# A fused attention and slot-router kernel: two thirds of the encoder's values multiplied behind the first tile, and the row sum moved to GpSimd

## The chip, the cores and the metric

One core of a Trainium2 chip runs the whole program. The metric is the device time of one execution in microseconds. Three executions of the kernel before were timed, and one execution was taken by the hardware profiler. TensorE (PE in the profile) multiplies matrices, VectorE (DVE), ScalarE (ACT) and GpSimd (POOL) work on tiles, SyncE (SP) issues most of the transfers. Each engine works through its own program in the written order and waits for the others only through semaphores.

## The reference

The inputs are 8 batches of 512 rows of 512 numbers (`x`), encoder rows of the same shape (`ctx`), a position `p` and a length for each batch. Everything is float32. Two residual blocks follow one another:

```python
# block 1: attention on a window of the encoder
h = (x - mean(x)) / sqrt(var(x) + 1e-5)
score = einsum('nqh,hk,nlk->nql', h, W_a, enc)
score = where(idx < max(p-16, 0) or idx > min(p+16, len), -1e9, score)
align = softmax(score) * exp(-(idx - p)**2 / 128)
context = einsum('nql,nlh->nqh', align, enc)
x = x + tanh(concat([context, h]) @ W_c.T)
# block 2: a router to 64 slots, on h2 = layernorm(x)
logits = (gelu(concat([h2, slot_mean]) @ w1 + b1) @ w2 + b2) / (abs(tau) + 0.1)
alpha  = softmax over the 8 largest logits, scattered into 64 slots
si     = einsum('bts,btd->bsd', alpha, h2) / (alpha.sum(1) + 1e-8)
S_new  = GRU(si, slots); attention among the slots; layernorm; @ wvp
x = x + einsum('bts,bsd->btd', alpha, slot_values) @ wo + bo
```

Only 36 encoder rows of a batch can count (34 of the window and two more columns for the case that nothing is masked in), so the kernel gathers these. In block 1 it multiplies the weights into the encoder once: `G` = window rows times `W_a`, so that a score is a product of `h` and `G`; and `EW` = window rows times the left half of `W_c`, times the Gauss weight, so that the context's part of the tanh is the product of softmax weights and `EW`. These are the encoder values of the title. The right half of `W_c` (`Wc2_raw`, which the profile calls Wc_raw) is multiplied with `h` directly, and since `h` has its mean taken off, the mean over the rows of this half is taken off the weights instead: `wcs` is the sum of its four pieces of 128 rows, and one product with a constant matrix `cmean` (-1/512 everywhere) gives minus the row mean for all partitions.

## The kernel before

The program is written by hand for each engine; no scheduler moves anything. Float32 products are made as three products of rounded parts: `mm3` multiplies high by high, low by high and high by low (the lines 456 to 458 of the profile). A high part is a rounding copy, usually on ScalarE; a low part is a subtraction of the high part from the full one, usually on VectorE (`..._lo`). The low parts that matter here are `WaT_lo` (weights of G, one operation for each of the four pieces of 128 rows), `Wc1T_lo` (weights of `EW`), `G_lo`, `GW_lo` (the second weights that a tile is multiplied with) and `EW_lo`.

Ahead of the tiles TensorE makes, in this order: the G products (48, piece k = 0 to 3 outermost, each k waits for `encWT` to say that `WaT_lo` of that piece is there), the product of the mean, and 36 products for `EW` in three groups `g` of 12. Group g holds the windows of batches 3g to 3g+2. VectorE meanwhile makes the `WaT_lo`, the three sums of `wcs`, the four `Wc1T_lo`, the four `G_lo`, adds the mean's product to the four pieces of `Wc2_raw`, splits the first tile (`low_x(0)`, the tile called hT_lo), and makes the four `GW_lo`.

Then come 32 tiles of 128 rows, in steps s = 0 to 31 on every engine. In step s TensorE makes the scores and the left half of the direct part (`score(s)`, 12 products with 292 columns), turns the softmax weights of tile s-1 (`turn_weights`, L1795), makes the right half (`right_half(s)`, 12 products with 256 columns), adds the context of tile s-1, does what `extras(s)` holds (in steps 1 to 6 the slots' own products) and turns the normalised rows of tile s-2 (`turn_rows`, L1770, which waits for `xh` of ScalarE). VectorE in step s takes the largest score, makes the statistics of tile s+3 (`stats1`), the softmax weights (`stack`), and the statistics of the new rows of tile s-1 (`stats2`). GpSimd adds the tanh to the row tile (`residual`), splits tile s+2 (`low_x`), makes the inverse deviations (`scales1`, `scales2`), and copies the four pieces of G of a batch beside the weights (`keys`). `w1` is the router's first weight matrix, which VectorE splits in step 1.

The semaphore `pre` counts what TensorE has finished ahead of the tiles. In the kernel before it stands at 1 after the hidden bias, at 2 to 5 after the four columns of G, at 6 after the mean and at 7 to 9 after the groups of `EW`. `EW` goes to its place for the context product by transfers: the first batch's three by ScalarE, after group 0, and the others by SyncE, which waits for `ew` to be 3, ahead of the loads of tiles 6 and later.

## Time and profile before

| | us |
|---|---|
| median of three executions | 347.88 |
| lowest and highest of them | 347.34, 349.73 |
| span of the profiled execution | 345.3 |
| TensorE busy (share of the span) | 328.8 (95%) |
| VectorE busy | 249.3 (72%) |
| ScalarE busy | 200.6 (58%) |
| GpSimd busy | 209.5 (61%) |
| mean granted TensorE clock | 0.992 of full |

The span runs from the first to the last instruction of the profiled execution. Its own device time is not listed apart from the three; by their median it would be the span and some 2.6 us around it. The start on the profile's clock is 0. In the rows below, a start and a duration are microseconds, `x4` says that four instructions stand in one row, and brackets at the end hold the idle time ahead of the row and what ended it.

### The profile page before, as it was taken

Reading aid. Unit: us, or ns where it says so; the run is one execution under the profiler, and the core shown is the slowest. Engines: PE = TensorE matmul, PEld = TensorE weight load, DVE = VectorE, ACT = ScalarE, POOL = GpSimd, SP = SyncE. Lnnn points to the kernel's source line nnn. Section 1 sums busy time; section 2 is a strip of 40 time slices with the busy share of each in tenths; the row PEclk is TensorE's granted clock in tenths of the full one; section 3 lists DMA queues with packets and bytes.
Section 4 is the critical chain, followed back from the end, with each engine's and each line's share of the span. In section 5 each row is a group of like instructions: output and inputs, shape, how many; then the busy total and the mean of one; then the engine's idle time right before and its main releaser. Section 6 shows DMA issues by size and latency. Waiting matters only on the chain.

```text
span 345.3 us, 7118 instructions
## 1 busy us (share of the span) xinstructions
PE 328.8 (95%) x2320; PEld 284.0 (82%) x2320; DVE 249.3 (72%) x749; ACT 200.6 (58%) x406; POOL 209.5 (61%) x353
## 2 busy tenths in 40 slices
PE   8999998999999999999999999989999999999980
PEld 6697856999898989989989989977889886777750
DVE  5589897666787777878877877766944765578872
ACT  3567226477759679578587777676853345323420
POOL 5600247879687876875885785737674336136772
PEclk9999999999999999999999999999999999999996
DMA  7999866242424242232232300009700000000898
GB/s 274 277 348 388 296 194 208 68 122 63 121 64 122 62 125 64 72 113 61 84 101 63 91 5 2 0 0 338 251 2 1 0 2 0 0 2 1 323 345 307
DMA packets 40934, 42.79 MB, mean 124 GB/s; under 512 B 3245, under 2 KB 32045, under 8 KB 40898
## 3 DMA queue, kind: packets, MB, share of 16 engines
q1 hardware_dynamic: 38944, 40.19, 35.2%
q10 hardware_dynamic: 1666, 1.49, 1.3%
q0 software_dynamic: 288, 0.66, 0.6%
q8 instruction: 19, 0.31, 0.4%
q14 instruction: 17, 0.14, 0.1%
HBM read 32.18 MB, written 8.39 MB: 117 GB/s over the span
## 4 chain that ended last, share of the span: by engine, by line
PE 57%; POOL 11%; DVE 9%; issue 8%; ACT 6%; DMA 6%; SPq 1%; POOLq 0%; ACTq 0%; DVEq 0%
PE psum L456 13%; PE psum L457 13%; PE psum L458 13%; PE psum L1741 4%; PE psum L2003 3%; POOL hT_lo L599 3%; DMA xT<-in_xT 3%; PE psum L1770 3%; DMA encw<-in_enc,rowi 2%; PE psum L1721 2%; POOL X L604 2%; ACT th L1320 2%; POOL r2all L610 1%; PE psum L1805 1%; PE psum L1952 1%
## 5 line engine op out<-in xcount | busy, mean ns | idle before, releaser
L456 PE MATMUL psum<-GW_hi,hT_hi 128*128 128x292 f32 (+1 forms) x256 | 78.5, 307 | 0.0
L458 PE MATMUL psum<-GW_lo,hT_hi 128*128 128x292 f32 (+1 forms) x256 | 73.9, 289 | 0.0
L457 PE MATMUL psum<-GW_hi,hT_lo 128*128 128x292 f32 (+1 forms) x256 | 73.9, 289 | 0.0
L604 POOL TENSOR_TENSOR X<-X,th 128x512 f32<-128x512 f32 x32 | 38.2, 1193 | 28.4 <-ACT th L1320 28.4
L456 PEld LDWEIGHTS psum<-GW_hi,hT_hi 128*128 128x128 f32 x256 | 48.4, 189 | 1.4 <-issue 1.2
L457 PEld LDWEIGHTS psum<-GW_hi,hT_lo 128*128 128x128 f32 x256 | 48.3, 189 | 0.0
L458 PEld LDWEIGHTS psum<-GW_lo,hT_hi 128*128 128x128 f32 x256 | 48.1, 188 | 0.0
L971 DVE BATCH_NORM_STATS2 st<-X 128x6 f32<-128x512 f32 x32 | 22.2, 693 | 26.7 <-POOL X L604 26.6
L599 POOL TENSOR_TENSOR hT_lo<-xT,hT_hi 128x512 fp32r<-128x512 f32 x30 | 39.1, 1304 | 2.0 <-DVE stack L982 2.0
L456 PE MATMUL psum<-xhT_hi,w_hi 128*128 128x256 f32 x128 | 37.9, 296 | 0.8 <-issue 0.5
L457 PE MATMUL psum<-xhT_hi,w_lo 128*128 128x256 f32 x128 | 36.1, 282 | 0.0
L458 PE MATMUL psum<-xhT_lo,w_hi 128*128 128x256 f32 x128 | 36.0, 281 | 0.0
L1307 ACT CAST aTs<-psum 108x128 fp32r<-108x128 f32 x32 | 8.6, 268 | 32.9 <-PE psum L1795 32.9
L1315 ACT ACTIVATE xh<-X,nm,r2all 128x512 f32<-128x512 f32 x31 | 25.1, 809 | 3.9 <-POOL nm L613 3.4
L456 PEld LDWEIGHTS psum<-xhT_hi,w_hi 128*128 128x128 f32 x128 | 24.2, 189 | 3.6 <-issue 3.4
L1301 ACT ACTIVATE e<-scm,nmr,rr 128x36 f32<-128x36 f32 x32 | 13.3, 417 | 20.0 <-DVE nmr L967 19.0
L457 PEld LDWEIGHTS psum<-xhT_hi,w_lo 128*128 128x128 f32 x128 | 24.3, 190 | 0.0
L458 PEld LDWEIGHTS psum<-xhT_lo,w_hi 128*128 128x128 f32 x128 | 24.3, 190 | 0.0
L456 PE MATMUL psum<-siT_hi,W_hi 128*128 128x256 f32 (+1 forms) x72 | 23.4, 325 | 0.0
L457 PE MATMUL psum<-siT_hi,W_lo 128*128 128x256 f32 (+1 forms) x72 | 23.1, 320 | 0.0
L458 PE MATMUL psum<-siT_lo,W_hi 128*128 128x256 f32 (+1 forms) x72 | 22.9, 318 | 0.0
L958 DVE TENSOR_TENSOR xhT_lo<-psum,xhT_hi 128x512 fp32r<-128x512 f32 x32 | 21.4, 667 | 2.0 <-ACT xhT_hi L1296 2.0
(316 smaller groups left out, 909.6 us busy)
## 6 DMA issues: line engine op xcount, KB each, us to landing
xT<-in_xT SPq DMA_DIRECT2D x32, 256.0 KB, 2.9
X<-in_x SPq DMA_DIRECT2D x32, 256.0 KB, 3.5
out<-ost SPq DMA_DIRECT2D x32, 256.0 KB, 3.0
WhhT<-in_WhhT SPq DMA_DIRECT2D x1, 3072.0 KB, 12.7
WihT<-in_WihT SPq DMA_DIRECT2D x4, 768.0 KB, 8.6
Wo<-in_wo ACTq DMA_DIRECT2D x4, 256.0 KB, 3.0
WvpT<-in_WvpT SPq DMA_DIRECT2D x4, 256.0 KB, 3.7
WaT<-in_WaT SPq DMA_DIRECT2D x1, 1024.0 KB, 11.1
```

Source lines behind the costliest of these rows:

```text
L456: pe.matmul(out, w_hi, m_hi, start=start, stop=False)
L457: pe.matmul(out, w_lo, m_hi, start=False, stop=False)
L458: return pe.matmul(out, w_hi, m_lo, start=False, stop=stop)
L599: pool.tensor_tensor(hT_lo[:, t % 2, :, :], xT[:, t % 4, :, :], hT_hi[:, t % 2, :, :].bitcast(F32), ALU.subtract).then_inc(S("hl"), 1)
L604: pool.tensor_tensor(tile_x(r), tile_x(r), halves(th[:, :]), ALU.add).then_inc(S("x2"), 1)
L958: v.tensor_tensor(xhT_lo[:, :, dst], bank.rearrange("p (c n) -> p c n", c=KC), xhT_hi[:, :, dst].bitcast(F32), ALU.subtract).then_inc(S("x ...
L971: link(v.bn_stats(st2[:, :], tile_x(r)), "stat")
L1301: act.activation(e[:, :], scm[:, :], ACT.Exp, bias=nmr[:, :], scale=rr1[:, s % 4:s % 4 + 1], accum_out=esum[:, :]).then_inc(S("ex"), 1)
L1315: act.activation(halves((th if r == NT - 1 else xh)[:, :]), tile_x(r), ACT.Identity, bias=nm2[:, :], scale=r2all[:, r:r + 1]).then_inc(S(" ...
L1741: last = pe.matmul(SI[h * NS:(h + 1) * NS, 0:XW], al, X[:, TPB * b + q, h, :], start=q == 0, stop=q == TPB - 1)
L1770: last = pe.transpose(bank[:, c * P:(c + 1) * P], rows_of[:, c * P:(c + 1) * P], ident[:, :])
L2003: last = pe.matmul(out_banks(m)[par], w[at_b, :], mv[g][at_b, :], start=n == 0, stop=n == 2)
```

## The change

Seven edits belong together.

1. TensorE makes the mean's product ahead of the last quarter of G. `pre` is therefore 2 after the mean and 3 to 6 after G's columns.
2. The three sums of `wcs` are made by GpSimd, which counts them in `row_sum`, followed by `low_x(0)`, which VectorE made.
3. VectorE adds the mean's product to `Wc2_raw` ahead of `G_lo`.
4. TensorE makes only group 0 of `EW` ahead of the tiles. Groups 1 and 2 (batches 3 to 7) are made in `extras(0)`, behind the right half of tile 0.
5. ScalarE and VectorE make `EW_hi` and `EW_lo` of these groups within step 0.
6. The wait for all of `GW_lo` ahead of step 0 is replaced by one for each piece within the first score.
7. ScalarE makes `w1_hi` at the end of its step 1, VectorE `w1_lo` in its step 2 (both were VectorE's in step 1).

```diff
-HB_DONE, G_DONE, WM_DONE, EW_DONE = 1, 1, KC + 2, KC + 2
+HB_DONE, WM_DONE, G_DONE, EW_DONE = 1, 2, 2, KC + 2
@@ gpsimd, behind the copy of bvz
+        pool.wait_ge(S("in_wc2"), 16)
+        pool.tensor_tensor(wcs[:, :], Wc2_raw[:, 0, :], Wc2_raw[:, 1, :], ALU.add).then_inc(S("row_sum"), 1)
+        for k in range(2, KC):
+            pool.wait_ge(S("row_sum"), k - 1)
+            pool.tensor_tensor(wcs[:, :], wcs[:, :], Wc2_raw[:, k, :], ALU.add).then_inc(S("row_sum"), 1)
+        low_x(0)
         pool.wait_ge(S("g_lo"), KC)
         keys(0)
@@ vector
-        v.wait_ge(S("in_wc2"), 16)
-        link(v.tensor_tensor(wcs[:, :], Wc2_raw[:, 0, :], Wc2_raw[:, 1, :], ALU.add), "rt")
-        link(v.tensor_tensor(wcs[:, :], wcs[:, :], Wc2_raw[:, 2, :], ALU.add), "rt")
-        v.tensor_tensor(wcs[:, :], wcs[:, :], Wc2_raw[:, 3, :], ALU.add).then_inc(S("v_prep"), 1)
@@
-        low_x(0)
@@ vector, extras
-            if s == 1:
-                v.wait_ge(S("in_w1"), 16)
-                link(v.tensor_copy(w1_hi[:, :, :], w1_raw[:, :, :]), "w1s")
-                link(v.tensor_tensor(w1_lo[:, :, :], w1_raw[:, :, :], w1_hi[:, :, :].bitcast(F32), ALU.subtract), "w1s")
+            if s == 2:
+                v.wait_ge(S("w1s"), 1)
+                v.tensor_tensor(w1_lo[:, :, :], w1_raw[:, :, :], w1_hi[:, :, :].bitcast(F32), ALU.subtract).then_inc(S("w1s"), 1)
@@ scalar, step
+            if s == 0:
+                high_values(1)
+                high_values(2)
+            if s == 1:
+                act.wait_ge(S("in_w1"), 16)
+                act.wait_ge(S("pre"), EW_DONE + NG)
+                act.copy(w1_hi[:, :, :], w1_raw[:, :, :]).then_inc(S("w1s"), 1)
@@ tensor
         for k in range(KC):
+            if k == KC - 1:
+                pe.wait_ge(S("row_sum"), ROW_SUM)
+                pe.wait_ge(S("wp"), KC)
+                pe.matmul(banks[7], cmean[:, :], wcs[:, :], start=True, stop=True).then_inc(S("pre"), 1)
@@
-        for g in range(NG):
+        def encoder_values(g):
@@
+        encoder_values(0)
+
         def extras(s):
 
+            if s == 0:
+                for g in range(1, NG):
+                    encoder_values(g)
@@ tensor, extras(2): the H1 bank; turn_rows(0): the trX bank
+                pe.wait_ge(S("ew"), 2)
+            if r == 0:
+                pe.wait_ge(S("ew"), NG)
@@ tensor, score
             for c in range(KC):
+                if s == 0:
+                    pe.wait_ge(S("split"), KC + c + 1)
@@
-        pe.wait_ge(S("split"), 2 * KC)
```

How the order changes on VectorE between `WaT_lo` and the first statistics: the tile names are the ones used above, and line numbers are those of each kernel. Before:

```order
L836 TENSOR_TENSOR wcs<-Wc_raw 128x512
L837 TENSOR_TENSOR wcs<-wcs,Wc_raw 128x512
L838 TENSOR_TENSOR wcs<-wcs,Wc_raw 128x512
L841 TENSOR_TENSOR Wc1T_lo<-Wc1T,Wc1T_hi 128x512 x4
L851 TENSOR_TENSOR G_lo<-psum,G_hi 128x288 x4
L856 TENSOR_TENSOR Wc_raw<-Wc_raw,psum 128x512 x4
L845 TENSOR_TENSOR hT_lo<-xT,hT_hi 128x512
L860 TENSOR_TENSOR GW_lo<-Wc_raw,GW_hi 128x512 x4
L864 SCALAR_TENSOR_TENSOR EW_lo<-psum,gw,EW_hi 108x512
L845 TENSOR_TENSOR hT_lo<-xT,hT_hi 128x512
```

The same place on VectorE in the changed kernel:

```order
L845 TENSOR_TENSOR Wc1T_lo<-Wc1T,Wc1T_hi 128x512 x4
L854 TENSOR_TENSOR Wc_raw<-Wc_raw,psum 128x512 x4
L859 TENSOR_TENSOR G_lo<-psum,G_hi 128x288 x4
L864 TENSOR_TENSOR GW_lo<-Wc_raw,GW_hi 128x512 x4
L868 SCALAR_TENSOR_TENSOR EW_lo<-psum,gw,EW_hi 108x512
L850 TENSOR_TENSOR hT_lo<-xT,hT_hi 128x512
```

The three sums and one `hT_lo` are gone, and the subtraction of the mean stands ahead of `G_lo`.

GpSimd behind its share of the weights of `Wp`. Before:

```order
L641 COPY bvz<-vecs 128x4
L585 COPY GW_hi<-G_hi 128x4x36
L586 COPY GW_lo<-G_lo 128x4x36
L593 TENSOR_SCALAR ve_168<-mr_167 128x2
L594 TENSOR_TENSOR rr_169<-ve_168,neghalf 128x2
```

GpSimd at the same place in the changed kernel:

```order
L643 COPY bvz<-vecs 128x4
L645 TENSOR_TENSOR wcs<-Wc_raw 128x512
L648 TENSOR_TENSOR wcs<-wcs,Wc_raw 128x512 x2
L601 TENSOR_TENSOR hT_lo<-xT,hT_hi 128x512
L587 COPY GW_hi<-G_hi 128x4x36
L588 COPY GW_lo<-G_lo 128x4x36
```

Four operations of 128x512 with two operands have come in ahead of the copies of `keys(0)`.

TensorE at the end of the encoder's products. Before, the last `G` product is followed by the mean, and the value products begin:

```order
L457 MATMUL psum<-encWT_hi,WaT_lo 128x288
L458 MATMUL psum<-encWT_lo,WaT_hi 128x288
L1624 MATMUL psum<-wcs,cmean 128x512
L456 MATMUL psum<-Wc1T_hi,encWT_hi 108x512
L457 MATMUL psum<-Wc1T_hi,encWT_lo 108x512
L458 MATMUL psum<-Wc1T_lo,encWT_hi 108x512
```

TensorE in the changed kernel, where group 0 of the values ends and the first tile's score begins:

```order
L458 MATMUL psum<-Wc1T_hi,encWT_hi 108x512
L459 MATMUL psum<-Wc1T_hi,encWT_lo 108x512
L460 MATMUL psum<-Wc1T_lo,encWT_hi 108x512
L458 MATMUL psum<-GW_hi,hT_hi 128x292
L459 MATMUL psum<-GW_hi,hT_lo 128x292
```

The score now follows after 12 value products, where it followed after 36, and the mean's product is no longer between G and the values.

## Rows read from the trace of the kernel before

**Rows 1.** The page, part 1: busy time, share and instructions of each engine.

```profile
PE 328.8 (95%) x2320; PEld 284.0 (82%) x2320; DVE 249.3 (72%) x749; ACT 200.6 (58%) x406; POOL 209.5 (61%) x353
```

**Rows 2.** Waits of TensorE from 20 to 64 us: total, times, longest.

```profile
PE psum L1770 <- ACT xh L1315: 1.2, 2, 1.0
PE psum L1795 <- DVE stack L982: 0.5, 1, 0.5
```

**Rows 3.** TensorE in order of time: start, duration, line, operation, out<-in.

```profile
20.91 0.38 PE L456 MATMUL psum<-encWT_hi,WaT_hi 128*128 128x288 f32 x1
...
27.36 1.02 PE L1624 MATMUL psum<-wcs,cmean 128*128 128x512 f32 x2
...
28.45 0.39 PE L457 MATMUL psum<-Wc1T_hi,encWT_lo 128*108 128x512 f32 x1
...
36.57 0.30 PE L456 MATMUL psum<-GW_hi,hT_hi 128*128 128x292 f32 x1
...
39.59 0.30 PE L456 MATMUL psum<-GW_hi,hT_hi 128*128 128x292 f32 x1
```

**Rows 4.** VectorE in order of time, 20 to 36 us, same columns.

```profile
21.23 0.74 DVE L810 SCALAR_TENSOR_TENSOR WaT_lo<-WaT,wneg,WaT_hi 128x512 fp32r<-128x512 f32 x1
...
24.73 0.69 DVE L838 TENSOR_TENSOR wcs<-wcs,Wc_raw 128x512 f32<-128x512 f32 x1
...
25.34 2.49 DVE L841 TENSOR_TENSOR Wc1T_lo<-Wc1T,Wc1T_hi 128x512 fp32r<-128x512 f32 x4
...
28.45 1.55 DVE L851 TENSOR_TENSOR G_lo<-psum,G_hi 128x288 fp32r<-128x288 f32 x4 [0.62 <-PE psum L1624]
...
29.92 2.47 DVE L856 TENSOR_TENSOR Wc_raw<-Wc_raw,psum 128x512 f32<-128x512 f32 x4
...
32.91 2.49 DVE L860 TENSOR_TENSOR GW_lo<-Wc_raw,GW_hi 128x512 fp32r<-128x512 f32 x4
```

**Rows 5.** ScalarE in order of time, 23 to 28 us.

```profile
23.95 2.19 ACT L1271 CAST Wc1T_hi<-Wc1T 128x512 fp32r<-128x512 f32 x4 [2.73 <-DMA Wc1T<-in_WcT]
...
26.08 0.62 ACT L1276 CAST hT_hi<-xT 128x512 fp32r<-128x512 f32 x1
```

**Rows 6.** The load of Wc_raw: its issue, and its row in the DMA issues.

```profile
15.17 0.37 SPq L494 DMA_DIRECT2D Wc_raw<-in_WcT  x1
...
Wc_raw<-in_WcT SPq DMA_DIRECT2D x1, 1024.0 KB, 5.5
```

**Rows 7.** VectorE beside GpSimd (POOL), at three later places.

```profile
242.65 0.43 DVE L1003 SCALAR_TENSOR_TENSOR kept<-kept,lsub 128x256 f32<-128x256 f32 x1
...
155.64 1.49 DVE L1003 SCALAR_TENSOR_TENSOR kept<-kept,lsub 128x256 f32<-128x256 f32 x1
...
155.56 1.29 POOL L599 TENSOR_TENSOR hT_lo<-xT,hT_hi 128x512 fp32r<-128x512 f32 x1
...
244.99 1.50 DVE L911 CAST W_hi<-WihT 128x512 fp32r<-128x512 f32 x1
...
246.16 1.46 POOL L660 TENSOR_TENSOR W_lo<-WihT,W_hi 128x512 fp32r<-128x512 f32 x1
```

**Rows 8.** VectorE from 41 to 51 us, and ScalarE's exponential of tile 3.

```profile
41.57 0.26 DVE L982 SCALAR_TENSOR_TENSOR stack<-e,ev,stack 128x36 f32<-128x36 f32 x1
...
48.00 1.81 DVE L929 CAST w_hi<-w_raw 128x1024 fp32r<-128x1024 f32 x1
...
49.84 1.23 DVE L930 TENSOR_TENSOR w_lo<-w_raw,w_hi 128x1024 fp32r<-128x1024 f32 x1
...
57.96 0.42 ACT L1301 ACTIVATE e<-scm,nmr,rr 128x36 f32<-128x36 f32 x1 [0.78 <-DVE nmr L967]
```

**Rows 9.** Busy time by stretch at the end; PEclk is 1.00 at 2.4 GHz.

```profile
core 0: us, PE busy (x) PEld busy (x) DVE busy (x) ACT busy (x) POOL busy (x), PEclk, DMA share, GB/s
337.00:339.00 2.00, 0.00 (x0) 0.00 (x0) 1.96 (x3) 0.69 (x1) 1.61 (x2) 1.00 1.04 392
340.00:345.00 5.00, 0.00 (x0) 0.00 (x0) 0.00 (x0) 0.00 (x0) 0.00 (x0) 0.50 0.68 263
```

More of the change, by code:

```diff
@@ L33 @@
 HT = T // 2
-HB_DONE, G_DONE, WM_DONE, EW_DONE = 1, 1, KC + 2, KC + 2
+HB_DONE, WM_DONE, G_DONE, EW_DONE = 1, 2, 2, KC + 2
 HI_WA, HI_ENC, HI_WC1, HI_G, HI_GW, HI_EW = 4, 4 + KC, 6 + KC, 6 + 2 * KC, 6 + 3 * KC, 6 + 4 * KC
 BVZ_DONE, LOW_WP = 5, 5
-SUMS_DONE, MEAN_DONE, CHUNKS_DONE, LOW_WC1 = 2, 3, 4, 4
+SUMS_DONE, MEAN_DONE, LOW_WC1 = 2, 3, 3
+ROW_SUM = 3
 SPLIT_WP = (2, 3)
@@ L844, in low_x @@
             v.wait_ge(S("hh"), t + 1)
+            v.wait_ge(S("hl"), t)
             v.tensor_tensor(hT_lo[:, t, :, :], xT[:, t, :, :], hT_hi[:, t, :, :].bitcast(F32), ALU.subtract).then_inc(S("hl"), 1)
+        v.wait_ge(S("pre"), WM_DONE)
+        for k in range(KC):
+            v.tensor_tensor(Wc2_raw[:, k, :], Wc2_raw[:, k, :], banks[7], ALU.add).then_inc(S("split"), 1)
         for c in range(KC):
@@ L851, in _ @@
             v.tensor_tensor(G_lo[:, c, :], src, G_hi[:, c, :].bitcast(F32), ALU.subtract).then_inc(S("g_lo"), 1)
-        v.wait_ge(S("pre"), WM_DONE)
-        for k in range(KC):
-            v.tensor_tensor(Wc2_raw[:, k, :], Wc2_raw[:, k, :], banks[7], ALU.add).then_inc(S("split"), 1)
-        low_x(0)
         for k in range(KC):
@@ L870, in _ @@
         stats1(1)
-        low_values(1)
         g3 = lambda a: a.rearrange("p (j s) -> p j s", s=NS)
@@ L1032, in step @@
                 scores_max(s)
-                if s == 0:
-                    low_values(2)
                 if live(s + 3) and s:
@@ L1039, in step @@
                     stats1(2)
+                    low_values(1)
             for b in range(NB):
@@ L1044, in step @@
                 stats1(3)
+                low_values(2)
             if s in TOPK_STEP:
@@ L1387, in _, with high_values @@
         act.wait_ge(S("first_row"), 1)
-        for g in range(NG):
-            if g == 2:
-                act.wait_ge(S("ew"), 1)
-                for k, part in enumerate((EW_hi, EW_hi, EW_lo)):
-                    act.dma_start(EW3[k * WS:(k + 1) * WS, 0, :].bitcast(F32),
-                                  part[0:WS, 0, :].bitcast(F32)).then_inc(S("ew3_first"), 16)
+        def high_values(g):
             act.wait_ge(S("pre"), EW_DONE + g + 1)
             act.activation(EW_hi[:, g, :], banks[4 + g][0:WP, :], ACT.Identity, scale=gw[0:WP, g:g + 1]).then_inc(S("wa"), 1)
+        high_values(0)
+        act.wait_ge(S("ew"), 1)
+        for k, part in enumerate((EW_hi, EW_hi, EW_lo)):
+            act.dma_start(EW3[k * WS:(k + 1) * WS, 0, :].bitcast(F32), part[0:WS, 0, :].bitcast(F32)).then_inc(S("ew3_first"), 16)
         for s in range(NT):
@@ L1620, in _ @@
                     last.then_inc(S("pre"), 1)
-        pe.wait_ge(S("v_prep"), CHUNKS_DONE)
-        pe.wait_ge(S("wp"), KC)
-        pe.matmul(banks[7], cmean[:, :], wcs[:, :], start=True, stop=True).then_inc(S("pre"), 1)
-        for g in range(NG):
+        def encoder_values(g):
             at_g = slice(g * WP, (g + 1) * WP)
```

## The prediction

> **What bounds the kernel now.** Read the shares of busy time first: TensorE is busy for 328.8 us of a span of 345.3 [rows 1]. Such a share says only that TensorE's work is nearly the whole time; what an edit is worth is decided by TensorE's idle time in the stretch that the edit touches. So I listed its waits from 20 to 64 us [rows 2]: three, 1.7 us in all. They are 0.5 us for the first tile's softmax weights and 1.2 us in two waits for the normalised rows `xh`, the longer one 1.0. Before 20.9 us the change moves nothing on TensorE, and it removes no product. The most that it can give back is therefore 1.7 us, 0.5%. What it can lose is open, because a step that had cover may lose it.
>
> Next, the order of time on TensorE [rows 3]. The products for G start at 20.91, one every (27.36 - 20.91) / 48 = 0.134 us. The mean's product starts at 27.36 and the 36 encoder value products follow, one every (36.57 - 28.45) / 35 = 0.232 us, which puts the mean's product at 28.45 - 0.23 - 27.36 = 0.86. The first score starts at 36.57 and step 0's 24 products end at 39.59, so they take 3.02 (score 1.61, right half 1.41). There is no idle time in all of this.
>
> Then VectorE over the same stretch [rows 4], where the columns to read are start and duration. It goes from one operation to the next, and its last `GW_lo` is done at 35.4, 1.2 us before TensorE comes to the score. The 8.4 us of encoder value products are the cover of this chain. That is the point on which the case turns.
>
> **The change part by part.**
>
> *24 of 36 value products behind the first tile.* The same work on TensorE, 24 x 0.232 = 5.57 us, comes later. TensorE now stands before the score at 36.57 - 5.57 = 31.0 and needs the four pieces of `GW_lo`. Time is won only where VectorE can deliver.
>
> *Row mean's product amid G.* It costs 0.86 on TensorE in either place. Three quarters of G end at 20.91 + 36 x 0.134 = 25.7, so the mean is there at 26.6 instead of 28.2, if the row sum is.
>
> *VectorE's chain without any disturbance.* The three sums of `wcs` (0.69 each, [rows 4]) leave. `Wc1T_lo` cannot use all of that: each piece waits for ScalarE's `Wc1T_hi`, which starts at 23.95 when the DMA lands and ends its fourth at 26.14 [rows 5]. The fourth low piece ends at 26.14 + 0.68 = 26.8 instead of 27.83. Then, with the spacings of [rows 4]: four subtractions of the mean (2.4) to 29.2, four `G_lo` (1.5) to 30.7, four `GW_lo` (2.4) to 33.1. `low_x(0)` (0.6) is gone from VectorE too. The last three products of the score then end at 33.1 + 0.4 = 33.5, the right half at 34.9, and the 24 value products at 40.5. In the kernel before, the same work is done at 39.59. So even here TensorE is 0.9 us later, since it waits some 2 us for `GW_lo` where it had cover.
>
> *The row sum on GpSimd.* `Wc_raw` lands at 15.17 + 5.5 = 20.7 [rows 6], and GpSimd is idle. A 128x512 addition of two SBUF operands takes 1.29 there [rows 7], so three end at about 24.6 undisturbed: in time for 25.7. But VectorE then has three `WaT_lo` to make (two SBUF operands, 0.74 each, from 21.23 on [rows 4]), for which the products of G wait. Rows 7 show what happens when both engines want this. `kept` on VectorE (two SBUF inputs, 256 elements) takes 0.43 alone at 242.65. At 155.64, begun 0.08 after a GpSimd subtraction, it takes 1.49 and ends 0.28 after that one does. Where both engines are back to back they alternate: VectorE's cast at 244.99 takes 1.50 through one GpSimd subtraction, and the GpSimd one at 246.16 takes 1.46 instead of 1.29, since it first waits for the cast. The operand in PSUM makes the difference: `encWT_lo`, `G_lo` and the mean's subtraction read one SBUF operand only.
>
> The Trainium skill (SBUF — State Buffer, "SBUF: two separate sides") says that the port pair shared by VectorE and GpSimd is an exclusive lock, held for a whole instruction, and that VectorE operations with two SBUF inputs take part in it. The trace agrees in rows 7 (1.49 for 0.43). By a split of the bandwidth, where each would slow in part, the sum below would be nearer to its undisturbed end.
>
> Worked out with this alternation (a blocked VectorE operation ends 0.6 after the GpSimd one, a blocked GpSimd one 1.13 after VectorE's; an estimate from rows 4 and 7): GpSimd's first sum 20.75 to 22.03; `WaT_lo` of piece 1 to 22.6; second sum to 23.8; piece 2 to 24.4; third sum to 25.5; piece 3 to 26.1. TensorE waits for these pieces 0.2 and 0.1 and runs the mean's product from 26.0 to 26.9, G to 28.5, and the values of batches 0 to 2 to 31.3. `low_x(0)` on GpSimd starts when ScalarE has `hT_hi` (26.7, [rows 5]) and falls among the four `Wc1T_lo`, which end at 29.65 instead of 26.8. Subtractions to 32.0, `G_lo` to 33.5. GpSimd's two `keys(0)` casts start then, again against `GW_lo`, and take turns with it: keys ready at 35.1, last `GW_lo` at 36.3. The score ends at 36.7, the right half at 38.1, the value products at 43.7. Against 39.59 that is **+4.1 us**, with TensorE idle from 31.3 to 35.1.
>
> Bounds of the collision: none is +0.9; if every GpSimd operation (three sums, `low_x(0)`, two casts) cost VectorE its full length, some 1.2 more than my count, it is +5.3. I take +4.1, since the rows with both engines back to back show full alternation.
>
> *What comes back.* TensorE is behind, the others less so, and the waits of [rows 2] shrink. The softmax weights of tile 0 (`stack`) are done at 41.8 now, 6.4 after the last `GW_lo` [rows 4, 8]; from 36.3 that is 42.7, and TensorE asks at 43.7 + 1.6 = 45.3, so 0.5 is gone. The router split: VectorE's `w_hi` takes 1.81 and `w_lo` 1.23 in step 1 [rows 8], just before the statistics on which the first `xh` waits. The cast goes to ScalarE (about 1.1 us, twice the 0.55 of a 512-wide one in [rows 5], in a step in which it waits), `w_lo` to step 2. The first `xh` wait, 0.2, goes. The second, 1.0, goes only in part: ScalarE makes that `xh` after the exponential of tile 3, which starts at 57.96 on VectorE's word [rows 8] and would by itself leave some 0.3 to 0.5, and `w_lo` now stands before the statistics of tile 1. I count 0.6. Together **-1.3 us**.
>
> *At nothing:* `EW_lo` of groups 1 and 2 later on VectorE, ahead of tile 1's score, covered by 5.57 us of value products. SyncE's wait for them delays the nine `EW3` transfers and the loads of tiles 6 on by some 5 us; their first users, in step 3, come later than the exponential of that step (57.96) and shift too, so I leave it at 0, with up to 0.5 if that slack is thin. The added waits on TensorE (`ew`) name work done long before.
>
> **Sum.** +4.1 - 1.3 = +2.8. From about 64 us on TensorE has no waits there that the change could reach, so the shift stays. On the profiled execution: 345.3 + 2.8 = 348.1 of span, with 2.6 us around it (347.88 - 345.3; the median of the three runs, which spread from 347.34 to 349.73). **Predicted: 350.7 us**, +0.8%. A measurement of this kernel can tell about 1% from no change.
>
> **The rivals.**
>
> *A, forecast, 0.42:* VectorE's chain becomes the bound and the lock adds to it. 349.8 to 351.5.
>
> *B, the clock falls, slower: 0.18.* In the gap 31.3 to 35.1 TensorE does nothing for 3.8 us. The rows at the end of the trace [rows 9] show TensorE without a product from 337 on, the granted clock at full up to 339 and at half from 340: it fell between 2 and 3 us into idleness. So it decides whether the gap is one unbroken wait of that length. Step 0's products (3.02) would then run at 1.2 GHz, some hidden behind `GW_lo`: +1.2 to +2.4 on A, 352.5. Against it: in the rest of the trace no wait of TensorE is over 1.0 us, so none shows how it behaves after a short gap. The Trainium skill (TensorE: Matmul & The Clock Gate, "Part 1: The HAM clock gate") has the same two levels and half rate for an idle engine; that is this rival's mechanism.
>
> *C, no collision or little of it: 0.27.* If the arbitration favours VectorE, or the sum on GpSimd falls into gaps, the shift is +0.9 to +1.9, less 1.3: 347.5 to 348.5. For it: `WaT_lo` and the sums overlap for under 4 us only. Against it: rows 7.
>
> *D, faster: 0.13.* VectorE delivers `GW_lo` by 32.2, when the score wants it. Then only the 1.3 to 1.7 us remain as gain: 346.4. It would take 0.9 us off the undisturbed chain; this is the most that the change can give, so faster by over 1% (under 344.4) has 0.02.
>
> Slower by over 1% (above 351.4) is B nearly whole and the upper edge of A: 0.26. The rest, 0.72, is within 1%. The range: the low end 347.2 takes in C, the high end 352.9 most of B and the upper bound of the collision; D and the top of B stay out.
>
> **What the profile of the changed kernel would show.** (1) VectorE's three later `WaT_lo` at 1.2 to 1.5 us instead of 0.74, between GpSimd sums of 1.3 to 1.7. (2) `Wc1T_lo` ending near 29.6, `GW_lo` near 36.3; by C near 33. (3) TensorE idle 3.5 to 5 us in all before and in the first score, waiting for the keys and `GW_lo`; by D none. (4) No wait for `stack` of tile 0, one `xh` wait of under 0.6. (5) Tile 0's value products ending near 43.7. (6) Clock full throughout; by B half for some microseconds near 35. Wrong it would be above all if two-operand VectorE work does not wait for GpSimd's as in rows 7, or if later steps give back more than TensorE's waits here allow.

## The result, and the profile after

| kernel | median of its executions, us | range | profiled span, us |
|---|---|---|---|
| before | 347.61 (4) | 347.29 to 349.73 | 345.3 |
| changed | 351.3 (4) | 350.74 to 351.87 | 348.9 |

The ratio is 1.0104, 95% interval 1.008 to 1.0127: slower by about 1%. The forecast was 350.7 us and the range reached to 352.9. The profiled execution took 350.74 us, so 1.9 us lie around its span.

Waits of TensorE from 20 to 70 us in the changed kernel, as in [rows 2]:

```profile
PE psum L458 <- POOL GW_lo L588: 2.3, 1, 2.3
PE psum L1787 <- ACT xh L1317: 0.3, 1, 0.3
```

The 1.7 us of [rows 2] are down to 0.3, and a wait of 2.3 us has come in at the first score. It ends when GpSimd's second cast of `keys(0)` is done; the name `GW_lo` stands there because a 36-column piece of that tile is what the cast writes. TensorE in order of time, as in [rows 3]: the mean's product, the start of the score, and the start of tile 1's score behind the value products:

```profile
29.24 1.02 PE L1620 MATMUL psum<-wcs,cmean 128*128 128x512 f32 x2
...
36.93 0.38 PE L458 MATMUL psum<-GW_hi,hT_hi 128*128 128x292 f32 x1 [2.32 <-POOL GW_lo L588]
...
45.61 0.30 PE L458 MATMUL psum<-GW_hi,hT_hi 128*128 128x292 f32 x1
```

VectorE, as in [rows 4]:

```profile
24.67 3.35 DVE L818 SCALAR_TENSOR_TENSOR WaT_lo<-WaT,wneg,WaT_hi 128x512 fp32r<-128x512 f32 x2
27.94 3.57 DVE L845 TENSOR_TENSOR Wc1T_lo<-Wc1T,Wc1T_hi 128x512 fp32r<-128x512 f32 x4
31.43 2.47 DVE L854 TENSOR_TENSOR Wc_raw<-Wc_raw,psum 128x512 f32<-128x512 f32 x4
33.82 1.54 DVE L859 TENSOR_TENSOR G_lo<-psum,G_hi 128x288 fp32r<-128x288 f32 x4
35.28 2.70 DVE L864 TENSOR_TENSOR GW_lo<-Wc_raw,GW_hi 128x512 fp32r<-128x512 f32 x4
```

GpSimd (POOL) beside it:

```profile
24.47 2.99 POOL L648 TENSOR_TENSOR wcs<-wcs,Wc_raw 128x512 f32<-128x512 f32 x2
28.77 1.58 POOL L601 TENSOR_TENSOR hT_lo<-xT,hT_hi 128x512 fp32r<-128x512 f32 x1 [1.31 <-ACT hT_hi L1278]
35.43 0.69 POOL L587 CAST GW_hi<-G_hi 128x144 fp32r<-128x144 f32 x1 [5.07 <-DVE G_lo L859]
36.07 0.76 POOL L588 CAST GW_lo<-G_lo 128x144 fp32r<-128x144 f32 x1
```

The reader is to see the stretching in pairs. Two `WaT_lo` take 3.35 us beside two sums. Four `Wc1T_lo`, 2.49 in [rows 4], take 3.57 beside the one subtraction `hT_lo`, and GpSimd's takes 1.58. The subtraction of the mean and `G_lo`, which read PSUM, have the lengths that they had before (2.47 and 1.54). The two casts of 144 elements are back to back, 0.69 and 0.76, each behind one `GW_lo`.

All of this came some 2 us later than the prediction has it. Busy time by stretch (PEclk is 1.00 at 2.4 GHz):

```profile
core 0: us, PE busy (x) PEld busy (x) DVE busy (x) ACT busy (x) POOL busy (x), PEclk, DMA share, GB/s
18.00:22.00 4.00, 4.00 (x15) 3.20 (x14) 3.15 (x9) 3.60 (x7) 0.00 (x0) 0.57 0.86 279
...
35.00:38.00 3.00, 1.07 (x8) 1.10 (x9) 3.00 (x6) 0.40 (x1) 1.41 (x2) 1.00 1.01 420
```

TensorE had waited 2.1 us for the encoder rows, which landed 1.9 us later than in the profile before (it begins to turn them at 17.21 against 15.29). It turned them and went on with the products of `Wo` and `Wvp`, and under these, from 18.5 to 21.9 us, its granted clock was at its lower level. G's products begin at 24.42 instead of 20.91. The change touches nothing there. A comparison by absolute times would charge this to the change, so I compare two lengths from here on: **a**, from the first product of G to the first of tile 1's score, and **b**, from there to the end of the span. The products inside a are the same in every kernel below but the filled one, since what is moved stays inside. A wait ahead of G's first product is not in a.

| profile | G starts | a | b | waits for keys, `GW_lo` or `WaT_lo` | half clock ahead of 60 us |
|---|---|---|---|---|---|
| before | 20.91 | 18.68 | 305.7 | none | none |
| changed | 24.42 | 21.19 | 303.3 | 2.3 | 18.5 to 21.9 |

So a is 2.5 longer and b 2.4 shorter, and the whole difference of the spans (3.6) is no more than the later start of G (3.5). This one pair of profiles can't say what the change costs.

### The profile page after: what moved, and what is told of

Read it like the earlier page. It is cut to its first block, busy times and chain, and to the rows that moved or that the text cites. A ratio compares the mean times of both kernels' runs of the same rounds, so it can differ in the third digit from the quotient of the medians.

```text
span 348.9 us, 7120 instructions
## 1 busy us (share of the span) xinstructions
PE 330.2 (95%) x2320; PEld 285.1 (82%) x2320; DVE 251.7 (72%) x744; ACT 202.2 (58%) x407; POOL 217.1 (62%) x357
## 4 chain that ended last, share of the span: by engine, by line
PE 66%; POOL 11%; issue 7%; ACT 6%; DVE 4%; DMA 3%; POOLq 0%; ACTq 0%; DVEq 0%
PE psum L458 16%; PE psum L459 15%; PE psum L460 15%; PE psum L1756 4%; PE psum L2021 3%; POOL hT_lo L601 3%; PE psum L1787 3%; DMA encw<-in_enc,rowi 3%; PE psum L1736 2%; PE psum L1824 2%; ACT th L1322 2%; POOL X L606 2%; POOL r2all L612 1%; PE psum L1655 1%; PE psum L1970 1%
## 5 line engine op out<-in xcount | busy, mean ns | idle before, releaser
L601 POOL TENSOR_TENSOR hT_lo<-xT,hT_hi 128x512 fp32r<-128x512 f32 x31 | 40.7, 1312 | 3.4 <-DVE stack L984 2.0
L458 PEld LDWEIGHTS psum<-xhT_hi,w_hi 128*128 128x128 f32 x128 | 24.2, 189 | 3.6 <-issue 3.4
```

The source lines that it names most:

```text
L458: pe.matmul(out, w_hi, m_hi, start=start, stop=False)
L601: pool.tensor_tensor(hT_lo[:, t % 2, :, :], xT[:, t % 4, :, :], hT_hi[:, t % 2, :, :].bitcast(F32), ALU.subtract).then_inc(S("hl"), 1)
```

## Experiments

**The theories.** *Chain:* VectorE's way to `GW_lo`, stretched by GpSimd, sets the start of the first score, since the 24 value products no longer cover it; the later split gives something back. *Clock:* the gap ahead of the score makes the granted clock fall, and this is the greater part. *Collision:* most of the loss is GpSimd's work beside VectorE's. *Start:* the profile's 3.5 us ahead of G are part of the cost. There are 6 to 12 executions of each kernel; ratios are to the kernel before in the same batch, whose medians were 347.73, 347.41 and 347.47 us (35, 20 and 22 executions). The three batches ran on three chips, so times are best compared within a batch.

### The kernel before, again

No edit.

> The kernel before, unchanged, once more: a second profile of it, to see how much of the 3.6 us between the two profiled spans is chance. In the profile of the changed kernel G starts at 24.4 us instead of 20.9, after encoder rows that landed 2 us later and 3.4 us of half clock from 18.5 on, all of it ahead of any edit. Theory 1 (chance of the start-up, common to both kernels): a second profile of the kernel before lands somewhere between the two, and its times scatter from 347 to 350. Theory 2 (the changed kernel has it always, for instance by its code's place): the kernel before again starts G near 20.9 with a full clock, and the median is within 0.3 us of 347.6.

Measured: 347.71 us, 1.0004 (0.9985 to 1.0023). In this profile G starts at 22.29, 1.4 later than in the profile before, with full clock; a is 19.15 and b 304.4. TensorE had waited 1.7 us for the encoder rows and VectorE 1.5 us for the load of `WaT`. So the start of G wanders by over a microsecond in an unchanged kernel. Its waits:

```profile
PE psum L1770 <- ACT xh L1315: 1.2, 2, 1.0
```

The 0.5 us for `stack` of [rows 2] are not there. They come in one execution of the kernel and not in the other. b differs by 1.3 us between these two profiles of one program.

### Row sum on GpSimd, alone

```diff
+        pool.wait_ge(S("in_wc2"), 16)
+        pool.tensor_tensor(wcs[:, :], Wc2_raw[:, 0, :], Wc2_raw[:, 1, :], ALU.add).then_inc(S("row_sum"), 1)
+        for k in range(2, KC):
+            ...
@@ vector
-        v.wait_ge(S("in_wc2"), 16)
-        link(v.tensor_tensor(wcs[:, :], Wc2_raw[:, 0, :], Wc2_raw[:, 1, :], ALU.add), "rt")
...
```

> The kernel before with one part alone: the three sums of the row mean on GpSimd. Theory lock: VectorE's last two or three WaT_lo and some Wc1T_lo take 1.2 to 1.9 us instead of 0.74 and 0.62, so G loses 0.2 to 0.6, but the 36 value products still cover VectorE's chain: 347.6 to 348.3. Rival (the sum on GpSimd is free, and VectorE wins 2.1 us for it): GW_lo is done 1 to 2 us earlier, WaT_lo keeps 0.74, time 347.2 to 347.6, as nobody waits for it.

Measured: 348.31 us, 1.0022 (1.0004 to 1.004); a 19.21, b 304.6, no new wait. VectorE and GpSimd where they meet:

```profile
23.68 3.41 DVE L815 SCALAR_TENSOR_TENSOR WaT_lo<-WaT,wneg,WaT_hi 128x512 fp32r<-128x512 f32 x2
27.02 2.48 DVE L842 TENSOR_TENSOR Wc1T_lo<-Wc1T,Wc1T_hi 128x512 fp32r<-128x512 f32 x4
```

```profile
21.86 1.29 POOL L643 TENSOR_TENSOR wcs<-Wc_raw 128x512 f32<-128x512 f32 x1 [4.66 <-DMA Wc_raw<-in_WcT]
23.22 3.33 POOL L646 TENSOR_TENSOR wcs<-wcs,Wc_raw 128x512 f32<-128x512 f32 x2
```

The two engines alternate: GpSimd's two sums take 3.33 and VectorE's two pieces 3.41, where they take 1.41 with GpSimd idle. VectorE loses the 2.0 us that it saves on the three sums. The value products cover this. Of the 0.6 us between the medians, 0.3 lie outside the span (2.2 us around it, in the kernel before of this batch 1.9).

### No GpSimd work in the changed kernel

```diff
@@ gpsimd
-        pool.wait_ge(S("in_wc2"), 16)
-        pool.tensor_tensor(wcs[:, :], Wc2_raw[:, 0, :], Wc2_raw[:, 1, :], ALU.add).then_inc(S("row_sum"), 1)
-        ...
-        low_x(0)
@@ vector, ahead of Wc1T_lo, and low_x(0) ahead of GW_lo
+        v.wait_ge(S("in_wc2"), 16)
+        v.tensor_tensor(wcs[:, :], Wc2_raw[:, 0, :], Wc2_raw[:, 1, :], ALU.add).then_inc(S("row_sum"), 1)
+        ...
+        low_x(0)
```

> The changed kernel with the row sum and low_x(0) back on VectorE, all else as changed (values of batches 3 to 7 behind the first tile, mean amid G, w1 later). Theory lock (GpSimd's work costs VectorE's chain 3 us, its own removal from VectorE saves 2.7): the last GW_lo comes at about the same time or up to 1.5 us earlier relative to the start of G, so 349.5 to 351.3. Rival (moving to GpSimd was a gain on the chain): it becomes slower than the changed kernel, 352 to 354.

Measured: 350.05 us, 1.0066 (1.0046 to 1.0087). Its waits:

```profile
PE psum L458 <- POOL GW_lo L588: 1.2, 1, 1.2
PE psum L458 <- DVE WaT_lo L812: 0.7, 1, 0.7
PE psum L1786 <- ACT xh L1316: 0.3, 1, 0.3
```

The 0.7 for `WaT_lo` stands ahead of G's first product: VectorE was late in this profile. `WaT_lo` and `Wc1T_lo` have their old lengths (1.40 for two, 2.49 for four), and yet most of the loss stays. Collision as the greater part falls. That the lost cover carries the loss is what the next kernel has to show.

### All values ahead in the changed kernel

```diff
-        encoder_values(0)
+        for g in range(NG):
+            encoder_values(g)
@@ extras(0)
-            if s == 0:
-                for g in range(1, NG):
-                    encoder_values(g)
```

> The changed kernel with all 36 value products ahead of the first tile again, all else as changed. Theory cover (the loss comes from TensorE standing before the first score without the 5.6 us of cover): TensorE has no wait before the first score, and the smaller waits of tiles 0 and 1 shrink by the later split of w1: 346.5 to 347.8. Rival (the loss comes from the lock and from G alone): 349.5 to 351.

Measured: 347.63 us, 0.9987 (0.9967 to 1.0006). All the collisions are still there (3.41 for two `WaT_lo`, 3.57 for four `Wc1T_lo`), the score's wait is gone, and with it the loss (b is 305.0: TensorE is early again, and waits 0.7 for `xh` and 0.4 for `stack`). Together with the kernel before it, this shows the lost cover as the necessary part: with the cover back the loss is gone with every collision in place, and without it the loss is there with those of the sums and of `low_x(0)` removed. The collisions are not free under cover, though. G's tenth product waits 0.5 for `hb`, which stands behind a stretched `WaT_lo` (1.15) on VectorE, and VectorE's later `GW_lo` is most likely what the 0.4 and 0.7 above come from, where the version with the split alone waits only 0.3 for `xh`.

### The changed kernel, again

No edit.

> The changed kernel, unchanged, in more executions. In the first four its mean clock was 0.986 to 0.991, while 30 of 35 executions of the kernel before had over 0.989. Theory B (the gap ahead of the first score invites a half-clock spell of 3.4 us, which costs about 1.5 us): half or more of the executions have a clock of 0.991 or less, and these are 1 to 2 us longer than the others; the fast ones are at 349.5 to 350.3. Theory A alone (a fixed loss of some 3 us, clock by chance as in the kernel before): one in six has a low clock, median 350.5 to 351.

Measured: 349.42 us, 1.0058 (1.004 to 1.0076), less than in the first measurement, whose interval (1.008 to 1.0127) it does not meet. The six executions, as time and mean granted clock of the span: 349.10 at 0.996, 349.11 at 0.995, 349.24 and 349.59 at 0.990, 350.52 at 0.987, 351.27 at 0.986. The four of the first measurement lay at 0.986 to 0.991. This pointed to the clock, but the profile had its 6.8 us of half clock from 22.4 to 29.2, ahead of the gap.

It begins within another wait, of G's first product for `WaT_lo`:

```profile
23.04 0.58 PE L458 MATMUL psum<-encWT_hi,WaT_hi 128*128 128x288 f32 x1 [1.67 <-DVE WaT_lo L818]
```

```profile
21.14 1.76 DVE L818 SCALAR_TENSOR_TENSOR WaT_lo<-WaT,wneg,WaT_hi 128x512 fp32r<-128x512 f32 x1
```

```profile
21.09 1.26 POOL L645 TENSOR_TENSOR wcs<-Wc_raw 128x512 f32<-128x512 f32 x1 [4.24 <-DMA Wc_raw<-in_WcT]
```

VectorE was nearly as late in the version with no GpSimd work (first `WaT_lo` at 21.40), and in that one the same wait is 0.7, with a `WaT_lo` of 0.74. The change itself adds the other 0.9 to 1.0: GpSimd's first sum starts 0.05 us ahead of the first `WaT_lo` and stretches it. This cost lies ahead of G and so is not in a; the prediction took this piece as made before the sums start.

### The gap filled with products

```diff
         encoder_values(0)
+        for _ in range(10):
+            pe.matmul(banks[5][0:WP, :], encWT_hi[:, 0, 0:WP], Wc1T_hi[:, 0, :], start=True, stop=True)
```

The ten products are extra work that nobody reads.

> The changed kernel with ten more products of 108x512 behind the first group of values, into a bank that is overwritten later; 2.3 us of TensorE work whose result nobody uses, in the place where TensorE waits. Theory B: the clock stays up, half-clock spells become as rare as in the kernel before, and the time falls by 0.5 to 1.5 to 350 or under. Theory A alone: nothing changes where the gap is 2.3 us or longer, and it grows by what the gap lacks: 351 to 352.

Measured: 349.83 us, 1.0077 (1.0054 to 1.01). The profile has full clock all the way to 341 and is therefore the best view of the chain alone. TensorE waits 0.8 for the keys, a is 22.46 with the fillers inside the old gap, b 303.3, the span 347.1. The time lies within what theory B expected, but against the changed kernel of the same batch (349.42) there is no gain by the medians. Against all 16 executions of the changed kernel (below) the median span is 1.1 us less (347.9 against 349.0). Six executions that scatter from 347.1 to 349.8 don't settle whether filling helps.

### Router split later, alone

```diff
@@ vector
-            if s == 1:
-                v.wait_ge(S("in_w1"), 16)
-                link(v.tensor_copy(w1_hi[:, :, :], w1_raw[:, :, :]), "w1s")
-                ...
+            if s == 2:
+                v.wait_ge(S("w1s"), 1)
+                v.tensor_tensor(w1_lo[:, :, :], ...).then_inc(S("w1s"), 1)
@@ scalar
+            if s == 1:
+                act.wait_ge(S("in_w1"), 16)
+                ...
+                act.copy(w1_hi[:, :, :], w1_raw[:, :, :]).then_inc(S("w1s"), 1)
```

> The kernel before with the split of w1 alone as in the change: the high part on ScalarE at the end of its step 1, the low one on VectorE in step 2. By the sum of the prediction 0.8 us of the two xh waits go (0.2 whole, 0.6 of the longer one) and the wait for the first softmax weights stays: 346.8 to 347.2. Rival: the wait is handed on, since w_lo now stands ahead of the statistics of tile 1, 347.4 to 347.9.

Measured: 346.37 us, 0.9975 (0.9955 to 0.9994). Its waits from 20 to 70 us:

```profile
PE psum L1773 <- ACT xh L1314: 0.3, 1, 0.3
```

b is 303.4, against 304.4 in the second profile of the kernel before: 1.1 us given back, 0.9 of it as `xh` wait. This edit is a small gain by itself, 1.0 us by the medians. The time is below the 346.8 to 347.2 expected, but the kernel before was itself 0.3 lower in this batch than in the last.

### One group of values behind

```diff
@@ the version with no GpSimd work
-        encoder_values(0)
+        for g in range(2):
+            encoder_values(g)
...
-                for g in range(1, NG):
+                for g in range(2, NG):
```

> The changed kernel with row sum and low_x(0) on VectorE and only the last group of values (batches 6 and 7) behind the first tile. TensorE then comes to the first score 2.8 us later than with both groups behind, at about the time that VectorE has the weights. Theory cover: the wait before the score shrinks from over 2 us to under 0.7, with it the half-clock spells, 347.2 to 348.3, at best as fast as the kernel before with w1 split later. Rival: any group behind the tile costs, and half of the loss stays: 348.8 or more.

Measured: 346.66 us, 0.9983 (0.9968 to 0.9999). Twelve products more ahead of the score (2.8 us), and its wait of 1.2 is gone; a is 19.21, b 303.5. The time is below the 347.2 to 348.3 expected. The last `GW_lo` ends 14.5 us after G's first product, with all of the two-operand work on VectorE.

### The changed kernel, a third time

No edit.

> The changed kernel once more, unaltered. Chain theory (VectorE's chain after the first tile's weights, stretched by the two adders on GpSimd, makes TensorE wait for keys and GW_lo): median between 349.1 and 351.3, one wait of 1.2 to 2.3 us for GW_lo or WaT_lo and an xh wait of 0.3 in the profile, wherever the half-clock spell lies. Clock theory (TensorE's clock falls because of the gap behind the first values): a half-clock stretch of over 1 us begins between the last product of the first values and the end of the right half of the first score, and the executions with a mean clock of 0.990 or less are 1.5 to 3 us longer than the others. If the spell again lies ahead of G's products or inside them, and the gap shows full clock, the clock theory is out.

Measured: 351.53 us, 1.0102 (1.0078 to 1.0125). Its profile shows what the two others didn't:

```profile
core 0: us, PE busy (x) PEld busy (x) DVE busy (x) ACT busy (x) POOL busy (x), PEclk, DMA share, GB/s
...
31.00:35.00 4.00, 1.01 (x5) 0.43 (x3) 4.00 (x9) 2.38 (x4) 1.33 (x2) 0.94 1.03 429
35.00:38.00 3.00, 2.83 (x12) 2.86 (x13) 3.00 (x5) 0.00 (x0) 0.07 (x1) 0.50 0.93 387
38.00:42.00 4.00, 4.00 (x19) 3.69 (x19) 1.77 (x9) 0.90 (x3) 1.17 (x3) 0.58 0.65 190
42.00:46.00 4.00, 4.00 (x19) 2.96 (x18) 2.61 (x7) 0.81 (x2) 1.30 (x1) 1.00 0.52 144
```

TensorE in order of time around it:

```profile
35.17 0.58 PE L458 MATMUL psum<-GW_hi,hT_hi 128*128 128x292 f32 x1 [3.17 <-POOL GW_lo L588]
35.55 0.45 PE L459 MATMUL psum<-GW_hi,hT_lo 128*128 128x292 f32 x1
35.80 0.45 PE L460 MATMUL psum<-GW_lo,hT_hi 128*128 128x292 f32 x1
36.04 0.45 PE L458 MATMUL psum<-GW_hi,hT_hi 128*128 128x292 f32 x1
...
41.74 0.39 PE L458 MATMUL psum<-Wc1T_hi,encWT_hi 128*108 128x512 f32 x1
41.97 0.39 PE L459 MATMUL psum<-Wc1T_hi,encWT_lo 128*108 128x512 f32 x1
```

The same stretch with the gap filled, full clock:

```profile
31.00:35.00 4.00, 3.30 (x15) 2.14 (x13) 4.00 (x9) 2.36 (x4) 1.36 (x2) 1.00 1.00 385
35.00:38.00 3.00, 2.85 (x23) 2.88 (x24) 3.00 (x5) 0.00 (x0) 0.05 (x1) 1.00 1.02 424
```

TensorE is idle from 32.0 to 35.2. At 34.5, 2.5 us into the gap, the clock goes to half and stays there to 41.3. The products of the first score come every 0.24 us instead of 0.13 (12 against 23 in the same 3 us). Here a is 25.32, with the chain like that of the filled version to 0.1 us: 25.32 - 22.46 = 2.9 us is what this spell of 6.8 us costs. The clock theory is no longer out, as it seemed from the two earlier profiles. It holds for this execution. Its other half does not: the executions with a mean clock of 0.990 or less (350.71 to 351.97) are not 1.5 to 3 us longer than the one above it (350.89). The median of 351.53 is also 0.2 above what the chain theory alone allowed.

### Row sum back on VectorE

```diff
@@ gpsimd (low_x(0) stays)
-        pool.wait_ge(S("in_wc2"), 16)
-        pool.tensor_tensor(wcs[:, :], Wc2_raw[:, 0, :], Wc2_raw[:, 1, :], ALU.add).then_inc(S("row_sum"), 1)
-        ...
@@ vector, ahead of Wc1T_lo
+        v.wait_ge(S("in_wc2"), 16)
+        v.tensor_tensor(wcs[:, :], Wc2_raw[:, 0, :], Wc2_raw[:, 1, :], ALU.add).then_inc(S("row_sum"), 1)
+        ...
```

> The changed kernel with the row sum alone back on VectorE (three additions of 0.7 us); the fourth part, low_x(0), stays on GpSimd. Collision theory: the two stretched WaT_lo pieces return from 3.35 for two to 1.4, and one stretched stretch is left, at Wc1T_lo beside low_x(0). VectorE's chain gains 1.9 us and loses 2.1 for the three additions, so TensorE's wait for keys and GW_lo stays at 1.5 to 2.5 us and the time at 350 to 351, no different from the changed kernel in the same batch by more than 0.5 us: moving the row sum to GpSimd is then worth nothing. Rival (the row sum's move is what costs): the wait falls by 1.5 us or more and the time is 348.3 or less.

Measured: 351.02 us, 1.0093 (1.0062 to 1.0125), beside 1.0102 (1.0078 to 1.0125) of the changed kernel. From G's first product to the score's first it is 13.92 us, in the changed kernel 13.87. The move of the row sum is worth nothing, as expected: what VectorE saves it waits away. Counted on VectorE, from the start of its first `WaT_lo` to the end of its last `GW_lo`, the move even costs 0.3 to 0.4 us: 15.85 here, 16.25 in the changed kernel and 16.16 in the filled one, whose second `WaT_lo` takes 1.20 and 1.10 instead of 0.74.

### `G_lo` first

```diff
@@ vector
-        v.wait_ge(S("pre"), WM_DONE)
-        for k in range(KC):
-            v.tensor_tensor(Wc2_raw[:, k, :], Wc2_raw[:, k, :], banks[7], ALU.add).then_inc(S("split"), 1)
         for c in range(KC):
             ...
             v.tensor_tensor(G_lo[:, c, :], src, G_hi[:, c, :].bitcast(F32), ALU.subtract).then_inc(S("g_lo"), 1)
+        v.wait_ge(S("pre"), WM_DONE)
+        for k in range(KC):
+            v.tensor_tensor(Wc2_raw[:, k, :], Wc2_raw[:, k, :], banks[7], ALU.add).then_inc(S("split"), 1)
```

> The changed kernel with the four G_lo ahead of the four subtractions of the mean on VectorE; nothing else. It asks which of the two ends the wait before the first score. If the keys (transposed with G_lo and cast on GpSimd) end it, they come 2.4 us earlier, the score starts when the last GW_hi and the first GW_lo are there, and 0.7 to 1.5 us come back: 348.5 to 349.5. If the chain to GW_lo ends it, which has the same length in either order, the wait only moves from ahead of the score into it and at most 0.3 us comes back: 349.5 to 350.5.

Measured: 350.64 us, 1.0091 (1.0064 to 1.0118), 0.9 below the changed kernel of the batch, with intervals that overlap, and above both expected ranges. Its wait and its casts:

```profile
PE psum L458 <- DVE GW_lo L864: 2.3, 1, 2.3
```

```profile
31.03 0.30 POOL L587 CAST GW_hi<-G_hi 128x144 fp32r<-128x144 f32 x1 [2.68 <-DVE G_lo L856]
31.28 0.31 POOL L588 CAST GW_lo<-G_lo 128x144 fp32r<-128x144 f32 x1
```

The casts take 0.30 beside the mean's subtraction, and the score starts 13.0 us after G's first product instead of 13.87. So in the changed kernel the keys do end the wait ahead of the score. But its nine products at full clock then come every 0.19 us, not every 0.13, behind the pieces of `GW_lo`: about half of the 0.9 goes there. This profile too has its half clock at the gap, 35.9 to 39.3, which begins 1.8 us after TensorE is back at work.

### Both small edits together

The version with one group behind, with `G_lo` first as above.

> The values of the first two groups ahead of the first tile, the third behind it; row sum and low_x(0) on VectorE; the mean's product amid G; the router weights' split one step later; G_lo ahead of the mean's subtraction. Chain theory: 2.8 us of value products cover more than the 1.2 us that TensorE waited in the version without GpSimd work, so no wait before the score, xh 0.3 left: 346.2 to 347.0, 0.2 to 0.4% below the kernel before. If moving value products behind the first tile costs something apart from the cover (a wait of ScalarE or of the first tile's values), the time is 347.5 or more.

Measured: 346.77 us, 0.9982 (0.9959 to 1.0005). No wait but the 0.3 for `xh`; a 19.23 and b 303.4, the numbers of the version without that edit. Under cover the order of `G_lo` is worth nothing. No version beats the split alone (0.9975); the intervals of the three overlap.

### The clock in all executions

| profile | G starts | a | b | wait for keys, `GW_lo`, `WaT_lo` | half clock ahead of 60 us | executions with a mean clock of 0.990 or less |
|---|---|---|---|---|---|---|
| before (all batches) | 20.91 | 18.68 | 305.7 | none | none | 13 of 77 |
| before, again | 22.29 | 19.15 | 304.4 | none | none | 2 of 12 |
| row sum on GpSimd, alone | 22.07 | 19.21 | 304.6 | none | none | 2 of 12 |
| split later, alone | 24.19 | 18.67 | 303.4 | none | 18.6 to 22.0 | 2 of 9 |
| all values ahead | 21.28 | 19.47 | 305.0 | none | none | 3 of 12 |
| one group behind | 20.86 | 19.21 | 303.5 | none | none | 2 of 12 |
| the same, `G_lo` first | 21.53 | 19.23 | 303.4 | none | none | 1 of 12 |
| gap filled | 21.34 | 22.46 | 303.3 | 0.8 | none | 2 of 6 |
| no GpSimd work | 22.29 | 22.64 | 303.3 | 1.9 | 24.2 to 27.6 | 7 of 12 |
| row sum back on VectorE | 21.46 | 22.59 | 303.5 | 1.7 | 23.2 to 26.6 | 6 of 11 |
| `G_lo` first | 21.10 | 23.75 | 303.3 | 2.3 | 35.9 to 39.3 | 6 of 6 |
| changed (all 16 executions) | 24.42 | 21.19 | 303.3 | 2.3 | 18.5 to 21.9 | 12 of 16 |
| changed, again | 23.04 | 22.89 | 303.5 | 2.9 | 22.4 to 29.2 | in the row above |
| changed, third | 21.30 | 25.32 | 303.5 | 3.2 | 34.5 to 41.3 | in the row above |

Of the waits, 0.7 with no GpSimd work and 1.7 in "changed, again" stand ahead of G and are not in a. The waits of 0.2 to 0.5 for `hb` inside G, in four profiles with the sums on GpSimd, are not listed.

The place of the spell matters. At the gap it lengthens a (25.32 and 23.75, against 22.46 with full clock). Inside G it hardly does (22.59 and 22.64 with 3.4 us of it, 22.89 with 6.8): TensorE comes later to the score and waits less there, since VectorE's chain has gone on meanwhile. Ahead of G it shows in G's start (24.42 and 24.19), together with the late rows. In the changed kernel a is 1.3 shorter, because VectorE was that much further when G began: its last `GW_lo` ends 13.6 us after G's first product instead of 14.9.

The last column is a rough sign only, since the mean takes in the idle end of the span as well, where the clock is at half in every kernel [rows 9]; the first profile of the changed kernel has a spell and a mean of 0.991. Still it separates: 12 of 69 executions of altered or repeated kernels with cover, 13 of 77 of the kernel before, 31 of 45 of those with an unfilled gap.

## Why the prediction was right, and which steps weren't

**The bound and the cover** were right, and are shown. Moving the 24 value products is what makes the loss: back ahead of the tile they take it away with every collision in place.

**The chain, +4.1.** The mechanism was right and the size nearly so. The prediction's own dates are 22.8 us from G's first product to tile 1's score (43.7 - 20.9). With full clock it is 22.46, in the filled version. In the third profile of the changed kernel the fourth `Wc1T_lo` ends 8.45 us after G's start, predicted 8.7, the last `GW_lo` 14.9, predicted 15.4, and the score starts at 13.9, predicted 14.2 (35.1). Against a of 18.7 to 19.2 in the kernel before, the loss is 3.3 to 3.8. It holds where the first `WaT_lo` is made before the sums start; in one profile of three it was not, and 0.9 to 1.0 us more came in ahead of G.

**The collision inside the chain.** The alternation was right for `WaT_lo` (two in 3.35 to 3.41, so 1.7 each where 1.2 to 1.5 stood in the text) and for `low_x(0)` (four `Wc1T_lo` in 3.57 instead of 2.49). What was wrong is the yardstick. I set the collision, 3.2 us, against a VectorE without sums, which nobody can have. Against VectorE making them itself the moves buy nothing and cost a little. From VectorE's first `WaT_lo` to its last `GW_lo` it is 16.25 us in the changed kernel, 15.85 with the row sum back, and 15.36 with `low_x(0)` back too (the version with one group behind, whose VectorE starts at the same 19.96): 0.9 in all, of the 3.3 to 3.8.

**What comes back, -1.3.** The size cannot be told apart from chance, and its make-up was off. The `stack` wait of 0.5 was counted as a gain, and the kernel before doesn't have it in its second profile. The `xh` waits give 0.9, where 0.8 was counted. From tile 1's score on, b falls from 304.4 and 305.7 to 303.3 to 303.5 with the split moved (305.0 where all values are ahead, with the waits named there): 1.1 by the one profile, 2.3 by the other. The edit alone measured 1.0 by the medians.

**The sum.** By the two executions of the changed kernel at 0.995 and 0.996 of full clock (349.1 us), against 347.4 in the median of the kernel before in that batch, the change with nearly full clock costs 1.7 us, not 2.8. That is two executions; the filled version's profile with full clock has about the same, 348.97. The time around the span was taken at 2.6, the median of three executions less the profiled span; where both numbers belong to one execution of these two kernels it is 1.8 to 2.1 (350.74 and 348.9 in the first). So of the 1.6 us between 350.7 and 349.1 some 0.7 is this term, and the rest the chain and what comes back.

**Rival B, 0.18, was dismissed too far; it is the step that failed.** The text had the clock fall "between 2 and 3 us into idleness", and a gap of 3.8 us in all, and yet point (6) says full clock throughout and the sum has nothing for it. In the third profile it falls 2.5 us into a gap of 3.2. The price was given as 1.2 to 2.4; it is 2.9 there. So it is partly luck that 350.7 came close to the 351.3 measured: the chain less the give-back makes some 349.1, and the executions above that go with a lower mean clock (12 of 16 at 0.990 or less). One profile shows the spell at the gap and two show it ahead. How much of the 2.2 us between 349.1 and 351.3 each makes is not measured. The range held, since it took in B.

**Of the points to look for:** (1) holds in kind; two of the three pieces took 1.7, more than was said. (2) holds in the third profile (29.8 and 36.2). (3): the wait at the first score is 1.2 to 3.2, where 3.5 to 5 was said; where the spell came ahead of the gap it took a part of it, and VectorE's chain was 0.5 shorter than forecast. (4) holds. (5): 43.8 in the filled version, 45.6 to 46.6 in the changed one. (6) is false in all three profiles, and its alternative (by B, half near 35) is true in one. "At nothing" was right: SyncE's loads of tile 6 went out at 55.5, and no wait of TensorE followed.

**What stays open.** In four of the seven profiles with a gap (the filled one counted) the half clock lies ahead of it, at 18.5 to 29.2 us, which no gap at 31 us can cause, and where it lies ahead it does not come again at the gap. Of seven profiles with cover one has it there. Part of this can be read from what TensorE did before. The two early spells (18.5 in the changed kernel, 18.6 in the split alone) follow the two longest waits for the encoder rows, 2.1 and 1.9 us; the other twelve profiles have 1.7 or less there and full clock. The one at 22.4 begins within the wait of 1.7 for `WaT_lo`, of which 1.0 is the change's own. The one at 24.2 comes after a wait of 0.7, the one at 23.2 after none since 15.9, and these two stay unexplained. Why kernels with a gap should have more low clocks in all, or how much of it is chance, no run here tells. Nor is it shown that filling the gap keeps the clock up: its six executions are too few, and a filled gap was seen with full clock once.

## What to carry to other kernels

Work of the bounding engine that stands ahead of a long chain of another engine is the chain's cover; before moving it, count the chain to its end at the place where the cover would stop, and add what a fall of the clock in the gap would cost (2.9 us here). Moving two-operand work from VectorE to GpSimd gained nothing here, and cost up to 0.9 us, while VectorE had such work of its own to do: weigh it against VectorE doing both. One profile has accidents of a microsecond or two at its start (here the landing of rows, a wait, the clock), so compare lengths between two landmarks around the edit, not absolute times, and profile the kernel before twice. Take the landmarks on the engine that the edit touches: counted from TensorE's first product of G, the cost on VectorE looked like 0.4, and a wait ahead of that product was missed.
